# Longer runs of one kind of matmul in a two-layer attention kernel's second layer, with the maxima's parts moved from VectorE to GpSimd

## What is computed

```python
q = split_heads(queries @ Wq.T)
k = split_heads(keys @ Wk.T)
v = split_heads(values @ Wv.T)
scores = jnp.einsum('bhqd,bhkd->bhqk', q, k) * scale
attn = jax.nn.softmax(scores, axis=-1)
ctx = jnp.einsum('bhqk,bhkd->bhqd', attn, v)
...
x = x + _L1_xattn_ref(_layernorm(x, axis=-1), ctx_1024, ctx_1024, ...)
x = x + _L1_ffn_ref(_layernorm(x, axis=-1), ...)
```

## Time and profile before

| | |
|---|---|
| median of 3 runs | 752.08 us (751.08 to 753.64) |
| the profiled execution | 753.41 us, span 751.6 us |
| granted PE clock, as a share of full speed | 0.999 |
| first layer and experts | 0 to about 531 us of the span |
| rounds of batches 1 to 13 in the second layer | 566.39 to 717.20 us |

### The profile page before, as it was taken

How to read it: one execution, slowest core, us unless ns; L and a number is a source line. 1 busy time by engine, 2 the same in 40 slices (tenths; PEclk the granted TensorE clock), 3 DMA queues, 4 the chain that set the end, 5 groups by cost and what they waited for, 6 DMA issues and landing times.

```text
span 751.6 us, 15540 instructions
## 1 busy us (share of the span) xinstructions
PE 726.8 (97%) x5784; PEld 561.3 (75%) x5784; DVE 474.8 (63%) x1106; ACT 312.4 (42%) x556; POOL 262.6 (35%) x266
## 2 busy tenths in 40 slices
PE   6989999999999999999999999999999999999996
PEld 4766667766766575699999998889777767777774
DVE  4678573457446578634444565738678968789735
ACT  1324211331143131235555555454246755565571
POOL 4984434242320433502210414123743324204041
PEclk9999999999999999999999999999999999999999
DMA  9799943532431395812443423354988765744101
GB/s 253 180 315 299 253 119 108 165 103 71 135 114 52 107 379 187 298 45 88 113 134 112 117 67 103 111 153 126 246 232 213 186 166 167 205 129 128 28 2 50
DMA packets 73068, 113.87 MB, mean 152 GB/s; under 512 B 14929, under 2 KB 59346, under 8 KB 71074
## 3 DMA queue, kind: packets, MB, share of 16 engines
q1 hardware_dynamic: 60928, 80.17, 37.2%
q10 hardware_dynamic: 5906, 17.03, 8.3%
q0 software_dynamic: 6160, 15.67, 6.6%
HBM read 84.27 MB, written 28.41 MB: 150 GB/s over the span
## 4 chain that ended last, share of the span: by engine, by line
PE 81%; DVE 8%; DMA 4%; POOL 2%; issue 1%; SPq 1%; ACT 1%; ACTq 0%; DVEq 0%; POOLq 0%
PE ps L1446 16%; PE ps L1081 12%; PE ps L1455 7%; PE ps L1096 7%; PE ps L2161 4%; PE ps L1115 4%; PE ps L2190 4%; DVE mxh L1796 4%; PE ps L1127 3%; PE ps L2181 3%; PE ps L1051 2%; PE ps L2154 2%; PE ps L1023 2%; PE ps L2135 2%; PE ps L1058 2%; DMA qst<-mT 2%
## 5 line engine op out<-in xcount | busy, mean ns | idle before, releaser
L1446 PE MATMUL ps<-rowsT,w 128*128 128x128 f32 x1120 | 130.8, 275 | 0.0
L1796 DVE TENSOR_REDUCE mxh<-ps 112x2 f32<-112x750 f32 x128 | 115.2, 931 | 21.9 <-PE ps L2161 20.2
L1446 PEld LDWEIGHTS ps<-rowsT,w 128*128 128x128 f32 x1120 | 128.0, 192 | 0.1
L2010 ACT ACTIVATE d_pT<-ps 125x448 f32<-125x448 f32 x192 | 93.2, 548 | 61.5 <-PE ps L2181 60.2
L1081 PE MATMUL ps<-x1T,sw 128*128 128x448 f32 x256 | 101.3, 540 | 0.0
L1400 ACT ACTIVATE w<-rw 128x1024 f32 x70 | 73.8, 1056 | 59.4 <-PE ps L1446 56.2
L1081 PEld LDWEIGHTS ps<-x1T,sw 128*128 128x128 f32 x256 | 47.5, 190 | 38.8 <-issue 35.9
L1339 POOL DMA_DIRECT2D yscr<-y x35 | 19.8, 564 | 154.5 <-DVE y L1373 154.4
L1455 PE MATMUL ps<-rw,h 128*128 x280 | 66.4, 380 | 0.0
L2161 PE MATMUL ps<-kst,qst 96*112 96x375 bf16 x256 | 63.7, 336 | 1.2 <-DVE heads L1823 0.8
L891 ACT ACTIVATE silu<-ps,sb 128x448 f32<-128x448 f32 x32 | 20.3, 634 | 96.9 <-PE ps L1081 96.9
(11 more groups left out here) (252 smaller groups left out, 1193.4 us busy)
## 6 DMA issues: line engine op xcount, KB each, us to landing
kst<-kscr SPq DMA_DIRECT2D x39, 378.0 KB, 5.3
rw<-in_rw SPq DMA_DIRECT2D x24, 512.0 KB, 9.5
kscr<-ka SPq DMA_DIRECT2D x16, 567.0 KB, 4.0
cT<-in_ctx_t SPq DMA_DIRECT2D x17, 378.0 KB, 4.8
ctxT<-in_ctx_t SPq DMA_DIRECT2D x16, 378.0 KB
ctxn<-in_ctx SPq DMA_DIRECT2D x16, 336.0 KB
qst<-qscr ACTq DMA_DIRECT2D x12, 448.0 KB, 6.8
rows<-xg SPq DMA_DIRECT2D x35, 128.0 KB, 2.8
```

What stands on the lines that cost most here:

```text
L1446: last = mm(bank[1 + 2 * q + k][:, block], w12[:, k, c, block], rowsT[:, q, c * P:(c + 1) * P], start=c == 0, stop=c == C - 1)
L1796: V.tensor_reduce(mxh[:, 2 * g:2 * g + 2], ps[0:S, p:p + 2, 0:K], axis=AX_X, op=ALU.max).then_inc(s["s_max"], 1)
L2010: A(pT[:, q % 2, k, :], bank[4 + k][0:KC, 0:QUAD * S], ACT.Exp).then_inc(s["p_ready"], 1)
```

## The change

- PE's order in the loop: `transposed` of a quad is one run of 12; `outputs` of two quads run together (0 and 1 in their batch, 2 and 3 in the next round); score pairs go two in a row, except around a block. The turn of the outputs stands right behind scores 0 and 1.
- `pair_uses`: three score pairs, not two, between the outputs' turn and the turn-over.
- ACT's order follows, and `pT` has three slots, not two. `xhL`, a buffer of the tail, now lies in `vt`'s memory.
- `parted` replaces `negated_parts`: the parts are no longer negated (the ones below the keys are minus ones instead), and from batch 2 on POOL makes them, each at a written place among its other work. `mxh` gets two slots.
- DVE's order: `finish` ahead of `turned`, and maximum 2 ahead of the row statistics.
- First layer: SP reloads the context's rows after `u_ps` alone, ahead of the wait for `v_ps`; `add_beta` of groups 0 and 1 is DVE's, no longer POOL's.

```diff
-TWO_ONES = 1.0 + 0x3F80 / 2.0 ** 23
+SLOTS = 3
+TWO_MINUS_ONES = -1.0 - 0xBF80 / 2.0 ** 23
...
         for j in range(G):
             sp.wait_ge(s["u_ps"], j + 1)
+            load_context_rows(1, j)
             sp.wait_ge(s["v_ps"], j + 1)
-            load_context(1, j)
+            load_context_T(1, j)
             keyed(j)
...
+    def add_beta(eng, i):
+
+        eng.wait_ge(s["xh_ready"], (i + 1) * G)
+        eng.tensor_tensor(x_res[:, i * G:(i + 1) * G, :], x_res[:, i * G:(i + 1) * G, :],
+                          beta_b[:].unsqueeze(1).to_broadcast([S, G, D]), ALU.add).then_inc(s["beta_added"], 1)
...
         input_stats(1)
+        v.wait_ge(s["small_in"], 16 * 6)
+        add_beta(v, 0)
         o_out(1)
         output_stat(1)
         keys(1)
         input_normalized(1)
         u_out(2)
+        add_beta(v, 1)
...
-            uses = ahead[0:2] + [("out", b - 1) if b else None] + ahead[2:4] + [("over", what, i) if what else None]
-            uses += ahead[4:7] + [("product", what, i) if what else None] + ahead[7:8]
+            uses = ahead[0:2] + [("out", b - 1) if b else None] + ahead[2:5] + [("over", what, i) if what else None]
+            uses += ahead[5:7] + [("product", what, i) if what else None] + ahead[7:8]
...
+    def parted(eng, b):
+
+        base, slot = b * 4, b % 2
+        eng.wait_ge(s["s_max"], b * 8 + 8)
+        if b >= 2:
+            eng.wait_ge(s["mT_ps"], b - 1)
+        eng.tensor_copy(mparts[:, slot, 0, :], mxh[:, slot, :]).then_inc(s["m_ready"], 1)
+        eng.wait_ge(s["m_ready"], base + 1)
+        eng.tensor_tensor(mr[:, slot, :], mxh[:, slot, :], mparts[:, slot, 0, :], ALU.subtract).then_inc(s["m_ready"], 1)
+        eng.wait_ge(s["m_ready"], base + 2)
+        eng.tensor_copy(mparts[:, slot, 1, :], mr[:, slot, :]).then_inc(s["m_ready"], 1)
+        eng.wait_ge(s["m_ready"], base + 3)
+        eng.tensor_tensor(mparts[:, slot, 2, :], mr[:, slot, :], mparts[:, slot, 1, :], ALU.subtract).then_inc(s["m_ready"], 1)
...
+            if j % 2:
+                parted(pool, j // 2 + 2)
             pool.wait_ge(s["p_ready"], (2 * j + 2) * NKC)
             gather(pool, i, j)
-        combine(i)
+        for j in range(0, G, 2):
+            combine(i, range(j, j + 2))
+            parted(pool, j // 2 + 4)
         rstd_of(pool, n, NORMS["q", i])
         normalized_beside(pool, i, NORMS["q", i])
-        pool.wait_ge(s["m_ready"], 4 * (G + 4))
+        parted(pool, 6)
+        parted(pool, 7)
         split_queries(pool, i)
         split_rest(pool, i)
-        for i in range(NG - 1):
+        parted(pool, 8)
+        for i, batches in enumerate(((9, 10, 11, 12), (13, 14, 15), ())):
             rstd_of(pool, n, NORMS["f", i])
             normalized_beside(pool, i, NORMS["f", i])
+            for b in batches[:1]:
+                parted(pool, b)
             add_bias(pool, i)
+            for b in batches[1:]:
+                parted(pool, b)
...
+            if g == 0 and b >= 2:
+                v.wait_ge(s["m_ready"], (b - 2) * 4 + 2)
             v.wait_ge(s["s_ps"], b * 8 + (g + 1))
             p = 2 * PAIR["score", b, g]
-            V.tensor_reduce(mxh[:, 2 * g:2 * g + 2], ps[0:S, p:p + 2, 0:K], axis=AX_X, op=ALU.max).then_inc(s["s_max"], 1)
...
+            if b:
+                finish(b - 1)
             turned(b + 1)
+            if ahead_of:
+                maximum(b + 2, 2)
             if kind == "q":
                 v.wait_ge(s["added"], 2 * G)
                 mean_var(v, n, k)
-            if b:
-                finish(b - 1)
             if ahead_of:
-                for g in range(2, 5):
+                for g in range(3, 7):
                     maximum(b + 2, g)
...
-                negated_parts(b + 2)
...
-            exps(b, 0, range(2))
+            exps(b, 0)
             if b:
                 keep_outputs(b - 1)
                 if b + 1 < NV:
                     load_values(b + 1)
-            exps(b, 0, range(2, NKC))
             exps(b, 1)
             if b in (G, 2 * G):
 
                 load_queries(a, b // G + 1)
             scaled(b, 0)
-            exps(b, 2, range(1))
             scaled(b, 1)
+            exps(b, 2)
             if what is not None:
                 turned_over(what, i)
-            exps(b, 2, range(1, NKC))
             scaled(b, 2)
-            exps(b, 3, range(1))
             scaled(b, 3)
+            exps(b, 3)
             if what == "q":
                 for m in range(C):
                     query_out(a, i, m, pair_bank(("product", what, i), m))
-            exps(b, 3, range(1, NKC))
...
-            if ahead_of:
-                arrived(b + 2)
-            if b:
-                score(0)
             t.wait_ge(s[f"mrow_in{b % 2}"], (b // 2 + 1) * 48)
             if b < 4:
                 t.wait_ge(s["ones_ready"], b + 1)
@@ -2258,31 +2270,34 @@
             elif b == NV:
                 t.wait_ge(s["va_ready"], 2)
             transposed(b, 0, range(2))
-            if b:
-                outputs(b - 1, 3)
-            else:
-                score(0)
-            score(1)
             if b == 0:
                 t.wait_ge(s["v_ready"], B)
             transposed(b, 0, range(2, NKC))
-
-            transposed(b, 1, range(2))
+            if b:
+                outputs(b - 1, 2)
+                outputs(b - 1, 3)
+            if ahead_of:
+                arrived(b + 2)
+            score(0)
+            score(1)
+
             if b:
                 t.wait_ge(s["outT_ready"], b)
+                t.wait_ge(*pair_read(EARLIER["out", b - 1]))
+                outputs_T(b - 1)
             else:
                 t.wait_ge(s["clear"], 1)
+            transposed(b, 1)
             maxima_T(b + 1)
-            if b:
-                t.wait_ge(*pair_read(EARLIER["out", b - 1]))
-                outputs_T(b - 1)
-            transposed(b, 1, range(2, NKC))
             score(2)
+            score(3)
+
+            transposed(b, 2)
+            if what is not None:
+                score(4)
             t.wait_ge(s["mT_ready"], b + 2)
             outputs(b, 0)
-            score(3)
-
-            transposed(b, 2, range(2))
+            outputs(b, 1)
             if what is not None:
                 t.wait_ge(*pair_read(EARLIER["over", what, i]))
                 if what == "o":
@@ -2290,14 +2305,12 @@
                 else:
                     t.wait_ge(s["xh_ready"], (NORMS[what, i] + 1) * G)
                 turn_over(what, i, heads[:, i * G:(i + 1) * G, :] if what == "o" else xh)
-            score(4)
-            outputs(b, 1)
+            else:
+                score(4)
             score(5)
-            transposed(b, 2, range(2, NKC))
-
-            transposed(b, 3, range(1))
+
+            transposed(b, 3)
             score(6)
-            transposed(b, 3, range(1, 2))
             if what is not None:
                 t.wait_ge(*pair_read(EARLIER["product", what, i]))
             if what == "q":
@@ -2306,9 +2319,7 @@
                 project("o", i, wo1, "o_ps")
             elif what == "f":
                 project("f", i, wf, "f_ps")
-            transposed(b, 3, range(2, NKC))
             score(7)
-            outputs(b, 2)
...
-        outputs(b - 1, 3)
         t.wait_ge(s[f"mrow_in{b % 2}"], (b // 2 + 1) * 48)
         transposed(b, 0)
+        outputs(b - 1, 2)
+        outputs(b - 1, 3)
...
-                ("d_pT", [KC, 2, NKC, GS], F32), ("outT", [P, 4, S], F32),
-                ("heads", [S, B, D], F32), ("xhL", [P, C, GS], F32), ("mxh", [S, NH], F32), ("mr", [S, 2, NH], F32),
+                ("d_pT", [KC, SLOTS, NKC, GS], F32), ("outT", [P, 4, S], F32),
+                ("heads", [S, B, D], F32), ("mxh", [S, 2, NH], F32), ("mr", [S, 2, NH], F32),
```

More of the change, by code:

```diff
@@ L1701, in gpsimd, with combine @@
     def gpsimd(pool, n):
-        def combine(i):
-            for j in range(G):
+        def combine(i, js):
+            for j in js:
                 for k in range(2):
@@ L2009, in exps @@
                 a.wait_ge(s["st_ps"], (b * 4 + q) * NKC + (k + 1))
-                A(pT[:, q % 2, k, :], bank[4 + k][0:KC, 0:QUAD * S], ACT.Exp).then_inc(s["p_ready"], 1)
+                A(pT[:, (b * QUAD + q) % SLOTS, k, :], bank[4 + k][0:KC, 0:QUAD * S], ACT.Exp).then_inc(s["p_ready"], 1)
         def keep_outputs(b):
@@ L2190, in outputs @@
                     last = mm(bank[7][32 * h:32 * h + HD + 1, q * S:(q + 1) * S], values[:, k, QUAD * q + h, :],
-                              pT[:, q % 2, k, h * S:(h + 1) * S], start=k == 0, stop=k == NKC - 1)
+                              pT[:, (b * QUAD + q) % SLOTS, k, h * S:(h + 1) * S], start=k == 0, stop=k == NKC - 1)
             if q == 3:
```

44 lines of the change are left out of this document (14 added, 30 removed).

## The result

The changed kernel takes 769.53 us (median of 4 runs, 768.03 to 771.89) beside 752.86 for the kernel before in the same session (751.08 to 754.43): a ratio of 1.0206, 95% interval 1.0175 to 1.0236. It is slower, by 16.7 us in the medians and by 14.6 us in the spans of the two profiled executions (766.2 and 751.6). Forecast were 9.3 more: 761.5 for the median, with 756 to 768 as the range, which the measured time exceeds by 1.5.

A forecast was written before the change was run, and what follows sets the result against it. PE, busy 97% of 751.6 us, was taken as the bound, with DVE nearly level. Terms +5.5, +5.0 and -1.2 gave +9.3: 761.5 us, forecast 758 to 765 (chance 0.63), range 756 to 768.

The forecast's parts named there:

- seven attention batches: Second layer's batches holding attention alone: 10.4 us each, 73.7 in all with batch 4's extra 0.9, against 68.23: +5.5.
- six block batches: Second layer's batches with a turn-over and a product: 14.6 us each against 13.76, +5.0 in all.
- tail: After the last scores, batch 14's outputs' turn stands right behind two quads and waits for ScalarE: +0.4 us.
- first layer: A cast's stall on DVE ends, but PE's next wait for a context load limits the gain: -1.2 us, bounds 0 and -3.5.
- The wait at the outputs' turn: Behind scores 0 and 1, PE waits for score 0's maximum: about 0.8 us new in each batch.
- The chain to 10.4: Attention batch, score 0 to next score 0, through waits for maxima: 10.4 us against 8.75 without waits, so PE waits 1.65.
- DVE works 8.3 of these 10.4: DVE's work in an attention batch: eight maxima of 0.92 plus 0.9 for the rest, 8.3 us of 10.4.
- Rival A: Maxima keep ahead and PE alone is the bound: attention batches 8.75 us, time 742; chance 0.07 for under 750.
- The maxima's rows by DMA: Between maxima's turn and next batch's turned scores, slack falls from 6.9 to 5.7 us; cost nothing, bounds 0 to 1.
- signs of being wrong: Outputs' turn not waiting, attention batches under 9.5 us, or waits at turned scores for the maxima's rows by DMA.
- Rival C: Dearer parts on GpSimd, or maxima's rows late by 0.5 us in each of 13 batches: 6.5 more, 768; chance 0.12.
- Parts hidden on GpSimd: Maxima's parts take 1.3 us on GpSimd, ready 1.9 us before the turn that needs them, so no cost.

The follow-up runs named there:

- Experiment 1: Second-layer maxima taken over 31 of 375 columns, exponentials' input scaled: in the changed kernel 754.28 us (1.0019), in the kernel before 749.93 us (0.9956).
- experiment 3: Changed kernel with the outputs' turn moved behind the next quad's turned scores and the maxima's turn: 764.96 us, 1.0136 to the kernel before.
- Experiment 5: Queries' load issued later, behind the rows of maxima, in the changed kernel: 767.29 us; issued earlier, ahead of the rows, in the kernel before: 758.14 us.
- Experiment 7: Changed kernel, queries' load late, tail's quads ahead of turned scores, ScalarE's copy first: 766.47 us. Kernel before, parts on GpSimd, queries late, batch 4's heads earlier: 753.43 us.
- experiment 6: First layer's edits alone in the kernel before: 755.13 us; changed kernel without them: 768.78 us; the latter with the queries' load late: 767.59 us.
- experiment 4: Maxima's parts on GpSimd in the kernel before: 751.63 us (0.9969); parts back on VectorE in the changed kernel: 773.19 us (1.0223).

## Why the prediction was right in direction and short in size

The slowdown was forecast, with its main mechanism, but the measured 769.53 lies above the whole range of 756 to 768. The spans' difference of 14.6 by the prediction's own terms:

| term | forecast | measured | from |
|---|---|---|---|
| seven attention batches | +5.5 | +7.75 | 75.98 - 68.23 |
| six block batches | +5.0 | +5.1 | 87.68 - 82.58 |
| batch 0 | -0.3 | 0 | 9.59 both |
| tail | +0.4 | +2.7 | 37.1 and 34.4 |
| first layer | -1.2 | -0.95 | start of batch 0, 555.85 and 556.80 |

The agreement of the block batches is partly luck. Five of them take 14.43, under the 14.6 forecast, and would give +4.0; batch 5 adds 1.1 by half clock, which was not forecast.

- **The wait at the outputs' turn**, "about 0.8 us in each batch": 0.82, 13 times, DVE's maximum as releaser. Experiment 1 shows the wait for the maxima as the cause of what the batches lose; experiment 3 shows that the place of the wait is not, since attention batches stay at 10.15 without it.
- **The chain to 10.4**: 10.35. "PE waits 1.65": with the row distances of the timeline a batch's work is 4 x 0.68 + 2 x 1.28 + 3 x 0.69 + 2 x 0.37 + 0.46 + 0.16 = 8.7, so 1.65 is left. The brackets show less (0.82 and 0.32); the rows' lengths reach past the next row's start (0.75 and 0.68 for twelve turned scores), so a part of the waiting counts as busy.
- **"DVE works 8.3 of these 10.4"**: 7.85. What it does beside the maxima was priced right (0.26 + 0.42 + 0.21 = 0.89 against 0.9). The eight maxima take 7.0 of its busy time and not 8 x 0.92 = 7.4: four in a row take 3.48.
- **Rival A**, PE as the bound, 742: even with the maxima nearly free the batch is 9.04, not 8.75, as ScalarE is next (experiment 1). So its price was wrong too.
- **The step that failed first**, and the largest, is "*The maxima's rows by DMA*": "Their turn moves from 6.9 us ahead ... to 5.7 ... I take nothing, with 0 to 1 us in batches 4 and 8 as bounds". I had the loss of slack, and let it cost nothing because the keys ahead in the queues moved as well. In batch 4 PE waited 0.88 already, the rows take 8.35 us there as before, and the lost 1.67 falls on PE whole; then comes half clock. Batch 4 takes 13.69 instead of the forecast 11.3, and batch 5 is 1.1 longer than its like: 3.5 us. Batch 8, for which I gave the same bounds, lost nothing. Experiment 5 takes away 3.1 of the 3.5 in the profiled execution and 2.2 in the medians, which are of two sessions. This was also one of my signs of being wrong ("if the wait stands at the turned scores with the rows' DMA as releaser"), but in one batch only.
- **The second is the tail**, "+0.4": I priced one wait for ScalarE. There are three, 0.76, 1.10 and 0.76, and twelve turned scores at 1.24: +2.7. Experiment 7 takes back 1.6 of it in its profile (22.14 to 20.50).
- **Rival C** had the rows in it and a time of 768, close to the measured one. That is luck: its price was 0.5 us in each of 13 batches, and the rows cost 3.5 us in one place, while nothing waited for the parts on GpSimd.
- **First layer**: the cast is back at 0.555 median and 1.527 at most, PE's wait for the context is 2.47 where I said 2.3. The gain of 1.2 is there in this one execution (0.95); over many it is not (experiment 6). A likely reason, not shown: the load's wait is 1.9 to 4.0 in the seven profiles with these edits, and in five of them a lowered clock follows (70 to 75 us, 0.66 to 0.79).
- **Parts hidden on GpSimd**: 0.28 apart, 1.1 together against my 1.3. Right, and in the old order they were a gain (experiment 4).

What stays open: 2.1 us between the spans' difference and the medians'. The profiled execution is the fastest of the four of the changed kernel, with a granted clock of 0.994; the others have 0.990 to 0.994 and no profile. And why the rows of batch 4 take 8 us at all: the keys' load stands ahead of them too, and no run moved it.

## What to carry to other kernels

Where two engines are nearly level and share two pairs of banks, handing over item by item keeps both busy. Longer runs can turn the lead of one into waits; here that was 1.2 us a batch, 0.82 of it in one place, where a maximum takes 0.92. A transfer that is waited for already has no slack: what moves its issue nearer to its use is paid in full (0.88 became 2.56 as 1.67 of slack went). And before a saving on the first engine is counted, ask which engine comes next: here ScalarE took 0.53 of the saving of about 0.6 a batch.
